# The triangular solve of a delta-rule recurrence: operand turned in 32x32 squares on VectorE instead of on TensorE, 32x64 tiles instead of 64x64, and the work around it reordered

## The chip, the cores and the metric

The kernel runs on one core of one Trainium2 chip. The metric is the device time of one execution in microseconds, as a median over runs. Beside it stands one profiled execution with its trace. All data is float32, apart from the routing tables.

## The reference

Two layers follow one another on an input x of 8 sequences x 512 steps x 256 channels (16 heads of 16).

```python
xx = pad(x)[:, :T] - x;  mix = x + xx * time_maa_x
lo = tanh(mix @ maa_w1) ...;  xm = x + xx * (lo @ maa_w2 + time_maa)      # four mixed inputs
r, k, v = xrg @ Wr.T, xk @ Wk.T, xv @ Wv.T                                  # and gates w, a, ma, mk, g
def step(s, (q, w, k, v, a, b)):            # s: 16x16 state per head and sequence
    sa = s @ a
    s = s * w + outer(sa, b) + outer(v, k)
    return s, s @ q
y = groupnorm(scan(step)) * ln_w + ln_b + (sum(r * k * faaaa)) * v
x1 = (y * g) @ Wo.T                          # first layer; the kernel adds x and normalises per token
# second layer: tokens are routed to 1 of 8 experts by argmax(x1 @ centroids.T);
# layernorm, relu(x W1[e] + b1[e]) W2[e] + b2[e], added to the token and written in token order
```

The scan is computed in blocks of 32 steps. Inside a block the effect of the steps on one another is a unit triangular 32x32 system per sequence and head (128 systems per block). Its inverse U is computed on GpSimd, and the solution X = U R is a set of small matrix products on TensorE, where R is what the state and the values contribute at each step.

## The kernel before

**Stages.** There are 16 blocks of 32 steps. `body(n)` is written once for each of the five engine queues and is called for n = -2 to 18. In one call it works on several blocks at once: projections and gates of block n+1, values of block n, solve, read-out and state update of block n-1, projection of the output and token statistics of block n-2, router of block n-3. After the loop the routing table is made, and the expert stage runs over 39 groups of 128 token slots. Each engine works strictly through its own list; the order on an engine is the order of the calls in its `body`, and engines wait for one another by semaphore counts.

**Names.** Channels lie in two halves f of 128 partitions; each half has four pairs of heads p (32 partitions each), and a group g is one half of one of the 8 sequences (16 groups). Two PSUM tensors `RY` (even and odd sequences) collect R and Y; six further PSUM banks are handed round by `Ring`: its list gives for each job the bank (`z@1` is job z in bank 1), and a job may start only when the job before it in that bank was read (`freed`).

**Around the solve.** TensorE's `read_state` puts R in `RY`. VectorE's `keep_r` copies it with a mask for even and odd heads to `Rm`; TensorE's `turn_r` turns it in 8 transposes of 128x128 (line 654); ScalarE's `keep_rt` copies the result to `RT`; `solve(m, f)` (line 699) multiplies, for each half f, 32 matrices `Ux` of 64x64 (two inverses on a block diagonal, zeros beside them) with 32 columns of `RT`. `keep_x` (ScalarE, line 1153) and `keep_x_odd` (VectorE, line 1505) copy X beside the values to `XV`, which `update` (line 716) and `read_out` (line 728) use.

**Around the inverse.** SyncE's `scores_to_pairs` writes the masked scores to DRAM (`scr_n`, line 462), loads them as one system per partition (line 467); GpSimd's `invert` works on them (it begins with the memset of line 1896); `inverse_to_heads` stores the result (`scr_u`, line 475) and loads it into `Ux` in four parts (line 486). Its place on SyncE is behind `store_x1` (line 452) and `load_tokens` (line 444).

**Around the scores.** VectorE's `mask_removal` (line 1467) and `mask_keys` (line 1436) fill `bkm` for all groups, then `difference` (1362) and `mix_stage` (1369) prepare the inputs of block n+2, then `keep_scores` (1489) reads each bank of scores. TensorE's `low_1` needs the mix, and `scores(n+1, 1)` goes into banks that `keep_scores` of the first half has to have read.

Of the kernel before, what the change touches and what calls it, by code (L numbers as in the profile page):

```python
# [143 lines left out]
def build(nc, d, out):  # L144
    with ExitStack() as ctx:
# [59 lines left out]
        def prm(name, h):  # L205
# [34 lines left out]
        Ux = [v.rearrange("p (f g k h t) -> p f g k h t", f=HALF, g=PAIRS, k=4, h=2)  # L240
              for v in (Ux_flat[:, 0:2048], Ux_flat[:, 2048:4096])]
        at_rm = top[0]
        Rm_flat = take(NB // 2 * P)
        Rm = Rm_flat.rearrange("p (g o h t) -> p g o h t", g=NB // 2, o=2, h=2)
        RT = [take(4 * P).rearrange("p (k n) -> p k n", k=4) for _ in range(HALF)]
# [37 lines left out]
        def within_words(v):  # L283
            at = [0]

            def some(words):
# [28 lines left out]
        nd = nc.dram_tensor("scr_n", (HALF, PAIRS, 4, 2, 2 * TB, TB), F32, kind="Internal").ap()  # L315
# [16 lines left out]
        proj = Stage(sem("proj"), [(1, "k z0 z1 a0 a1 sg ma0 ma1 abs sq sab mk0 mk1 ln lnss inv W ek iW0 iW1 v "  # L332
                                        "vm0 vm1 tg")])
        comb = Stage(sem("comb"), [(1, "kk scan t f k2 ls e2 kkn q ao bt k3 rk bm0 bm1 km0 km1 u wend")])
# [8 lines left out]
        chain_dve = Stage(sem("chain_dve"), [(-1, "rme rmo x1o x0o")])  # L343
        state_dve = Stage(sem("state_dve"), [(-1, "sa s")])
        chain_act = Stage(sem("chain_act"), [(-1, "rt1 rt0 x1e x0e ye yo")])
# [8 lines left out]
                 "r": [(comb, "rk"), (comb, "q")], "v": [(proj, "v"), (proj, "vm1")], "kk": [(comb, "kk")], "ss": [(comb, "bm1")],  # L354
                 "rk": [(comb, "u")], "rt0": [(chain_act, "rt0")], "rt1": [(chain_act, "rt1")], "su": [(state_dve, "s")],
# [6 lines left out]
        freed.update({f"x{f}": [(chain_act, f"x{f}e"), (chain_dve, f"x{f}o")] for f in range(HALF)})  # L362
        filled = [sem(f"filled{i}") for i in range(len(banks))]
        ring = Ring(banks, [(0, "bk00@5"), (1, "h@2 k@3"), (0, "bk01@2"), (1, "z@1 a@4 kk@5"), (-3, "logit@2"),
# [40 lines left out]
        block = ctx.enter_context(nc.Block())  # L405
        x_rows_of = lambda e: slice(64 * (1 - e), 64 * (1 - e) + 64)
# [4 lines left out]
        def _(sp):  # L411
            w = Waits(sp, carrier)

            early = [(masks, d["masks"]), (mats, d["mats"].rearrange("m p n -> p m n"))]
# [40 lines left out]
            def scores_to_pairs(m):  # L455
# [3 lines left out]
                for f in range(HALF):  # L459
                    score.wait(sp, m, *(f"sc{f}{p}" for p in range(PAIRS)))  # L460
                    for e in range(2):
                        sp.dma_start(nd[f, :, :, e].rearrange("g k r t -> r g k t"),
                                     sc[m % 2][x_rows_of(e), f, :, :, e, 0, :]).then_inc(n_out, 16)
# [3 lines left out]
                sp.dma_start(Up[m % 2].rearrange("p r c -> p (r c)"),  # L467
                             nd.rearrange("f g k e (h s) t -> (f g k e h) (s t)", h=2)).then_inc(n_in, 16)

            def inverse_to_heads(m):  # L470
# [5 lines left out]
                if m == last:  # L476
                    load_tokens(last)
                sp.wait_ge(u_out, (m + 1) * 16)
                if m == 0:
                    sp.wait_ge(clear_ok, 1)  # L480
                if m >= 2:
                    ring.wait_full(sp, m - 2, "x0", "x1")
                for e in range(2 if m < last else 1):
                    for h in range(2):
                        at_row = 64 * (1 - e) + TB * h
                        sp.dma_start(Ux[m % 2][at_row:at_row + TB, :, :, :, h, :], u_rows[e, h]).then_inc(u_in, 16)

            u_rows = ud.rearrange("(f g k e h) (r c) -> e h r f g k c", f=HALF, g=PAIRS, k=4, e=2, r=TB)
# [1528 lines left out]
```

## Time and profile before

| | us |
|---|---|
| median of 3 runs | 1094.39 |
| lowest and highest | 1082.82, 1096.72 |
| the profiled execution | 1087.63 |
| its span, first to last instruction | 1085.4 |

In that execution TensorE (PE) is busy for 93% of the span, VectorE (DVE) for 72%, GpSimd (POOL) for 57% and ScalarE (ACT) for 50%. The loop over blocks takes the time to about 750 us, the expert stage the rest.
### The profile page before, as it was taken

What the parts mean: (1) busy time and instruction counts of PE and PEld (TensorE: products, weight loads), DVE (VectorE), ACT (ScalarE), POOL (GpSimd) and SP (SyncE); (2) the same over time, 40 slices, a digit from 0 to 9 for tenths busy, and PEclk for the clock granted to TensorE, in tenths of its full rate; (3) what the DMA queues carried; (4) which work ended last, traced back from release to release, by engine and by line L of the source; (5) the groups of instructions that cost most, each with busy time, mean ns of one, the idle gap of its engine ahead of it and who ended that gap; (6) DMA issues with size and microseconds to landing.
All of it is one profiled execution on the core that took longest, in us unless ns stands there. A gap on an engine that the chain in (4) does not pass through costs nothing.

```text
span 1085.4 us, 42536 instructions
## 1 busy us (share of the span) xinstructions
PE 1010.8 (93%) x16804; PEld 833.9 (77%) x16805; DVE 777.0 (72%) x1777; ACT 542.0 (50%) x1113; POOL 614.4 (57%) x1135
## 2 busy tenths in 40 slices
PE   8898999999999999999999999499899999999995
PEld 5676777787777787777777777477799888989894
DVE  4776788788887887888788777157467666666663
ACT  4475677686685685776766766122122222222220
POOL 1088786787687885876867868820223232333321
PEclk9999999999999999999999999689999999999998
DMA  4113224234134133243242242828555454545430
GB/s 110 42 20 79 72 43 99 58 56 110 40 73 109 27 86 87 37 99 82 41 100 59 54 101 44 234 63 289 182 182 181 148 185 150 189 144 182 150 125 4
DMA packets 208752, 112.15 MB, mean 103 GB/s; under 512 B 172364, under 2 KB 192080, under 8 KB 208208
## 3 DMA queue, kind: packets, MB, share of 16 engines
q1 hardware_dynamic: 202208, 100.90, 34.4%
q0 software_dynamic: 3744, 8.40, 2.3%
q8 instruction: 122, 2.00, 0.8%
q10 hardware_dynamic: 2640, 0.54, 0.3%
q14 instruction: 38, 0.31, 0.1%
HBM read 85.55 MB, written 26.08 MB: 103 GB/s over the span
## 4 chain that ended last, share of the span: by engine, by line
PE 78%; DMA 7%; DVE 6%; issue 5%; ACT 1%; SPq 1%; POOL 1%; DVEq 1%; POOLq 0%; ACTq 0%
PE bank L561 19%; PE bank L950 12%; PE bank L963 9%; PE bank L646 6%; PE bank L699 6%; PE bank L654 5%; PE ry L963 4%; PE bank L607 3%; PE ry L676 2%; PE ry L728 2%; PE bank L716 2%; DMA arena<-scr_n 2%; DMA scr_n<-arena 2%; DMA arena<-scr_u 2%; DVE arena L1489 1%
## 5 line engine op out<-in xcount | busy, mean ns | idle before, releaser
L1906 POOL TENSOR_TENSOR arena<-arena 128x30 f32<-128x30 f32 (+14 forms) x480 | 263.5, 549 | 37.6
L561 PE MATMUL bank<-arena 128*128 128x256 f32 (+2 forms) x992 | 266.5, 406 | 5.9 <-DVE arena L1405 2.5
L1903 POOL TENSOR_TENSOR arena<-arena 128x30 f32<-128x30 f32 (+14 forms) x480 | 249.9, 521 | 36.4
L561 PEld LDWEIGHTS bank<-arena 128*128 128x128 f32 x992 | 172.7, 196 | 50.9 <-issue 24.7
L950 PEld LDWEIGHTS bank<-arena 128*128 128x128 f32 x1248 | 146.9, 194 | 5.5 <-issue 2.7
L950 PE MATMUL bank<-arena 128*128 128x128 f32 x1248 | 147.4, 277 | 3.1 <-DVE arena L1812 2.5
L1489 DVE TENSOR_TENSOR arena<-bank,arena 128x512 f32<-128x512 f32 x128 | 79.5, 682 | 32.8 <-PE bank L646 32.8
L1293 ACT ACTIVATE arena<-arena 128x1 f32<-128x1 f32 x39 | 11.5, 295 | 177.2 <-DVE arena L1766 177.2
L963 PE MATMUL bank<-arena 128*128 x416 | 96.4, 385 | 0.0
L1937 POOL COPY arena<-arena 128x1 int32 (+1 forms) x39 | 7.1, 183 | 146.2 <-DVE arena L1830 146.2
L963 PEld LDWEIGHTS bank<-arena 128*128 128x128 f32 x416 | 76.9, 190 | 14.4 <-issue 4.8
L699 PEld LDWEIGHTS bank<-arena 64*64 64x64 f32 x2048 | 65.3, 140 | 24.2 <-issue 16.7
L654 PE MATMUL bank<-arena 128*128 128x128 f32 x560 | 80.9, 281 | 2.0 <-issue 0.9
L699 PE MATMUL bank<-arena 64*64 64x32 f32 x2048 | 68.5, 224 | 14.2 <-DMA arena<-scr_u 12.1
L654 PEld LDWEIGHTS bank<-arena 128*128 128x128 f32 x560 | 64.9, 143 | 19.3 <-issue 13.6
L646 PE MATMUL bank<-arena 32*128 32x64 f32 x2048 | 69.0, 275 | 9.4 <-issue 8.5
L1931 POOL DMA_INDIRECT arena<-scr_x,arena x39 | 41.2, 1056 | 61.1 <-POOL arena L1929 30.4
L646 PEld LDWEIGHTS bank<-arena 32*128 32x128 f32 x2048 | 63.8, 188 | 13.7 <-issue 11.5
L1380 DVE SCALAR_TENSOR_TENSOR bank<-bank,arena 128x256 f32<-128x256 f32 x128 | 56.1, 483 | 22.4 <-PE bank L579 22.4
L1896 POOL MEMSET arena<- 128x32 f32 x16 | 2.5, 157 | 121.1 <-DMA arena<-scr_n 121.1
L1812 DVE TENSOR_SCALAR arena<-bank,arena 128x128 f32<-128x128 f32 x156 | 44.0, 344 | 23.1 <-issue 18.0
L1939 POOL DMA_INDIRECT out_dram<-arena x39 | 39.8, 1021 | 34.9 <-DVE arena L1796 20.8
(174 smaller groups left out, 1799.2 us busy)
## 6 DMA issues: line engine op xcount, KB each, us to landing
arena<-in_W SPq DMA_DIRECT2D x47, 1024.0 KB, 5.0
scr_n<-arena SPq DMA_DIRECT2D x64, 128.0 KB, 3.0
arena<-scr_n SPq DMA_DIRECT2D x16, 512.0 KB, 3.9
scr_u<-arena SPq DMA_DIRECT2D x16, 512.0 KB, 2.9
arena<-scr_u SPq DMA_DIRECT2D x62, 128.0 KB, 2.8
arena<-in_xTp SPq DMA_DIRECT2D x32, 132.0 KB, 4.1
arena<-in_x SPq DMA_DIRECT2D x64, 64.0 KB, 2.1
scr_x<-arena SPq DMA_DIRECT2D x64, 64.0 KB, 2.5
```

Of the source, the lines that this page charges most:

```text
L561: mm = pe.matmul(ring.tile(m, name)[0:rows, to], lhsT, rhs, start=(i == 0), stop=(i == len(terms) - 1))
L646: mm = pe.matmul(ring.tile(m, f"sc{f}{p}")[:, b * 2 * TB:(b + 1) * 2 * TB], bkm[r, f * B + b, :], aq[m % 2][r, f * B + b].rearrange("p x t ...
L654: mm = pe.transpose(ring.tile(m, name)[:, i * P:(i + 1) * P], src, ident)
L699: mm = pe.matmul(ring.tile(m, f"x{f}")[x, at:at + 32], Ux[m % 2][x, f, p, k].rearrange("p h t -> p (h t)"), RT[f][x, k, 32 * p:32 * p + 32 ...
L950: mm = pe.matmul(hidT_ps[t // 4][:, (t % 4) * P:(t % 4 + 1) * P], W1[s][:, k, t * P:(t + 1) * P], xnT[:, k, :], start=(k == 0), stop=(k == ...
L963: mm = pe.matmul(y_ps[s][:, 0:D], hidT[s][:, t, :], W2f[:, bass.ds(e * (FT * D) + t * D, D)], start=(t == 0), stop=(t == FT - 1))
L1380: xm_ok.inc(m, f"{g}{h}", STT(out=part, in0=part, scalar=prm(f"maa{g}", h), in1=dx[:, h], op0=ALU.add, op1=ALU.mult))
L1489: score.inc(m, name, TT(sc[m % 2][:, f, p].rearrange("p k e x t -> p (k e) (x t)"), ring.tile(m, name)[:, :].rearrange("p (b n) -> p b n", ...
L1812: relu_dve.inc(str(t), nc.vector.tensor_scalar(hidT[s][:, t], hidT_ps[1][:, (t - 4) * P:(t - 3) * P], b1f[:, bass.ds(e * FT + t, 1)], 0.0, ...
L1903: inv_ok.inc(f"m{s}", TT(t, U[:, 0:s, s:s + 1].broadcast_to(shape), U[:, s:s + 1, s + 1:TB].broadcast_to(shape), ALU.mult))
L1906: inv_ok.inc(f"a{s}", TT(U[:, 0:s, s + 1:TB], U[:, 0:s, s + 1:TB], t, ALU.add))
L1931: nc.gpsimd.indirect_dma_start(out=xg[:, s], out_offset=None, in_=x_rows, in_offset=bass.IndirectOffsetOnAxis(ap=index, axis=0), bounds_ch ...
```

## The change

- **R.** `keep_r` is now two VectorE transposes that turn each 32x32 square of R where it stands, into `Rs`. `turn_r`, `keep_rt`, `Rm` and `RT` are gone.
- **Solve.** `solve(m, w)` now multiplies matrices of 32 rows and 64 columns (two inverses side by side) with 32 columns of `Rs`; the products of a head with the other head's R also arise, and are masked when X is copied. Two pairs of heads are worked on in each call, alternately into banks `xa` and `xb`; both are complete only after `solve(m, 1)`. There are again 64 matmuls per block.
- **Copies of X.** Three VectorE multiplications with a mask, and two ScalarE copies with a scale of 0 or 1; `x_kept` waits for all of them.
- **Order and banks.** `gates`, then a and kk ahead of z, `ma_mk` ahead of the router; both parts of the solve behind `project_out`, with `norms` between them. `Ring` has other banks.
- **Masked keys** are written for each half apart, and the scores and the transposes of keys of a half wait for that half alone.
- **SyncE** stores the inverse first, then issues the token loads, then the loads of the inverse, then the store of x1 of block n-3.

TensorE's list, from the second transposes of keys to the first read-out of X, in a middle block. Before (L607 is z, a, kk, ma, mk; L769 a filling matmul; L561 128x8 the router, x2 behind it the gates; L654 x8 `turn_r`; L561 x4 `project_out`; L699 the solve; L561 128x512 `norms`; then r, keys, v):

```order
L607 MATMUL bank<-arena 128x256 x6
L769 MATMUL bank<-arena 128x256
L561 MATMUL bank<-arena 128x8 x4
L561 MATMUL bank<-arena 128x256 x2
L607 MATMUL bank<-arena 128x256 x4
L654 MATMUL bank<-arena 128x128 x8
L561 MATMUL bank<-arena 128x256 x4
L699 MATMUL bank<-arena 64x32 x32
L561 MATMUL bank<-arena 128x512
L561 MATMUL bank<-arena 128x256 x4
L699 MATMUL bank<-arena 64x32 x32
L654 MATMUL bank<-arena 128x128 x12
```

Now:

```order
L572 MATMUL bank<-arena 128x256 x2
L618 MATMUL bank<-arena 128x256 x10
L789 MATMUL bank<-arena 128x256
L572 MATMUL bank<-arena 128x8 x4
L572 MATMUL bank<-arena 128x256 x4
L714 MATMUL bank<-arena 64x32 x32
L572 MATMUL bank<-arena 128x512
L714 MATMUL bank<-arena 64x32 x32
L572 MATMUL bank<-arena 128x256 x4
L666 MATMUL bank<-arena 128x128 x12
```

The eight transposes are gone; the second part of the solve moved from behind r, keys and v to ahead of them, with one 128x512 matmul between the two parts.

VectorE's list, from the key exponent to the scores. Before (L1505 the copies of X, L1467 and L1436 the masks, L1362 and L1369 the inputs of the next block, L1489 the scores):

```order
L1505 COPY arena<-bank 64x4x128
L1403 SCALAR_TENSOR_TENSOR arena<-arena 128x512
L1405 SCALAR_TENSOR_TENSOR arena<-arena,bank 128x512
L1425 TENSOR_TENSOR arena<-bank,arena 128x512
L1505 COPY arena<-bank 64x4x128
L1467 TENSOR_TENSOR arena<-bank,arena 128x8x2x32 x2
L1436 TENSOR_TENSOR arena<-arena 128x8x2x32 x2
L1369 SCALAR_TENSOR_TENSOR arena<-arena 128x256 x2
L1489 TENSOR_TENSOR arena<-bank,arena 128x512 x4
```

Now:

```order
L1411 SCALAR_TENSOR_TENSOR arena<-arena 128x512
L1413 SCALAR_TENSOR_TENSOR arena<-arena,bank 128x512
L1512 TENSOR_TENSOR arena<-bank,arena 64x2x8x32 x3
L1433 TENSOR_TENSOR arena<-bank,arena 128x512
L1477 TENSOR_TENSOR arena<-bank,arena 128x4x2x32 x2
L1445 TENSOR_TENSOR arena<-arena 128x4x2x32 x2
L1377 SCALAR_TENSOR_TENSOR arena<-arena 128x256 x2
L1499 TENSOR_TENSOR arena<-bank,arena 128x512 x4
```

Between the rows shown stand others that did not change. The two copies of X, one ahead and one behind, became three in one place, and each mask is now written in two pieces (the second pair, like the first, is not shown).

SyncE's list, one block, before and now:

```order
L462 DMA scr_n<-arena 64x16x32 x4
L467 DMA arena<-scr_n 128x1024
L452 DMA scr_x<-arena 32x2x256 x4
L444 DMA arena<-in_x 32x2x256 x4
L475 DMA scr_u<-arena 128x1024
L486 DMA arena<-scr_u 32x32x32 x4
```

```order
L474 DMA scr_n<-arena 64x16x32 x4
L479 DMA arena<-scr_n 128x1024
L487 DMA scr_u<-arena 128x1024
L456 DMA arena<-in_x 32x2x256 x4
L498 DMA arena<-scr_u 32x32x32 x4
L464 DMA scr_x<-arena 32x2x256 x4
```

The store of the inverse now stands directly behind the load of the next systems. The core of the diff:

```diff
+        Rs = take(NB * TB).rearrange("p (e g i) -> p e g i", e=2, g=NB // 2)
+        head_mask = take(TB + 2)
...
-        ring = Ring(banks, [(0, "bk00@5"), (1, "h@2 k@3"), (0, "bk01@2"), (1, "z@1 a@4 kk@5"), (-3, "logit@2"),
-                            (-2, "g@0"), (1, "ma@5 mk@2"), (-1, "rt0@3 rt1@4"), (-2, "wo@0"), (-1, "x1@1"),
-                            (1, "ss@0 r@4"), (0, "bk11@5"), (1, "v@2"), (-1, "x0@3"), (0, "bk10@5 v0@1 v1@4"),
-                            (1, "rk@3"), (-1, "su@0"), (1, "sc00@2 sc01@5 sc02@3 sc03@1 tg@4"), (2, "lo1@5"),
+        ring = Ring(banks, [(0, "bk00@5"), (1, "h@2 k@3"), (0, "bk01@2"), (-2, "g@4"), (1, "a@5 kk@3 z@1 ma@4 mk@2"),
+                            (-3, "logit@3"), (-2, "wo@0"), (1, "ss@0"), (-1, "xa@1 xb@3"), (1, "r@4"),
+                            (0, "bk11@5"), (1, "v@2"), (0, "bk10@5 v0@1 v1@3"),
+                            (1, "rk@4"), (-1, "su@0"), (1, "sc00@2 sc01@5 sc02@3 sc03@1 tg@4"), (2, "lo1@5"),
...
+            def solve(m, w):
+                if w == 0:
+                    for bank in "ab":
+                        ring.wait_empty(pe, m, f"x{bank}")
+                    chain_dve.wait(pe, m, "re", "ro")
+                    pe.wait_ge(u_in, (m + 1) * 64)
+                else:
+                    pe.wait_ge(half_solved, m + 1)
+                for g in range(NB // 2):
+                    for turn in range(2):
+                        for i, bank in enumerate("ab"):
+                            e, r = (turn + i) % 2, pair_rows(2 * w + i)
+                            at = (w * NB // 2 + g) * 32
+                            mm[bank] = pe.matmul(ring.tile(m, f"x{bank}")[x_rows_of(e), at:at + 32],
+                                                 Ux[m % 2][r, g % 4, g // 4, e].rearrange("p h t -> p (h t)"), Rs[r, e, g, :],
+                                                 start=True, stop=True)
...
             def keep_r(m):
...
                 for e, name in enumerate("eo"):
-                    chain_dve.inc(m, f"rm{name}", TT(Rm[:, :, 1 - e], RY[e][:, :, 0, None, :].broadcast_to(shape),
-                                                     odd_even[:, None, :, None].broadcast_to(shape), ALU.mult))
+                    chain_dve.inc(m, f"r{name}", nc.vector.transpose(Rs[:, e], RY[e][:, :, 0]))
+            def keep_x(m, bank, e):
+                ring.wait_full(dve, m, f"x{bank}")
+                chain_dve.inc(m, f"x{bank}{'eo'[e]}", TT(solution_home(m, "ab".index(bank), e), solution(m, f"x{bank}", e),
+                                                         same_head[x_rows_of(e), None, None, :].broadcast_to([P // 2, 2, NB // 2, 32]),
+                                                         ALU.mult))
```

## Rows read from the trace of the kernel before

**Rows 1.** A block by engine: busy PE, PEld, DVE, ACT, POOL; PEclk, DMA share, GB/s.
```profile
333.00:373.40 40.40, 39.10 (x919) 31.42 (x918) 34.75 (x61) 29.58 (x55) 31.36 (x60) 1.00 0.33 74
```

**Rows 2.** Time line of GpSimd: where the inverses of block 1, of a middle block and of the last begin.
```profile
90.34 0.16 POOL L1896 MEMSET arena<- 128x32 f32 x1 [1.85 <-DMA arena<-scr_n]
...
342.18 0.16 POOL L1896 MEMSET arena<- 128x32 f32 x1 [4.57 <-DMA arena<-scr_n]
...
679.41 0.15 POOL L1896 MEMSET arena<- 128x32 f32 x1 [3.17 <-DMA arena<-scr_n]
```

**Rows 3.** Time line of TensorE in one block, 332 to 374 us.
```profile
332.02 1.12 PE L561 MATMUL bank<-arena 128*128 128x512 f32 x2
...
348.70 1.09 PE L654 MATMUL bank<-arena 128*128 128x128 f32 x8
...
351.45 2.06 PE L699 MATMUL bank<-arena 64*64 64x32 f32 x64
...
361.83 0.76 PE L728 MATMUL ry<-arena 128*32 128x32 f32 x64
...
365.16 0.68 PE L728 MATMUL ry<-arena 128*32 128x32 f32 x54 [0.69 <-issue]
...
370.54 2.01 PE L646 MATMUL bank<-arena 32*128 32x64 f32 x62
...
373.41 1.12 PE L561 MATMUL bank<-arena 128*128 128x512 f32 x2
```

**Rows 4.** Groups of TensorE by line and shape, 119 to 680 us: busy, mean ns, idle before.
```profile
L646 PE MATMUL bank<-arena 32*128 32x64 f32 x1728 | 59.0, 275 | 9.1 <-issue 8.5 <-DVE arena L1489 0.3
L699 PE MATMUL bank<-arena 64*64 64x32 f32 x1664 | 53.4, 220 | 2.4 <-DMA arena<-scr_u 2.4
L728 PE MATMUL ry<-arena 128*32 128x32 f32 x1664 | 21.2, 199 | 5.7 <-issue 5.7
```

**Rows 5.** Time line of VectorE in the same block.
```profile
343.48 1.28 DVE L1499 TENSOR_TENSOR arena<-ry,arena 128x512 f32<-128x512 f32 x2
...
354.35 0.92 DVE L1403 SCALAR_TENSOR_TENSOR arena<-arena 128x512 f32<-128x512 f32 x1
...
355.92 0.69 DVE L1452 SCALAR_TENSOR_TENSOR bank<-bank,arena 128x512 f32<-128x512 f32 x1
...
360.49 0.68 DVE L1505 COPY arena<-bank 64x512 f32<-64x512 f32 x1 [0.47 <-PE bank L699]
361.09 1.27 DVE L1467 TENSOR_TENSOR arena<-bank,arena 128x512 f32<-128x512 f32 x2
362.29 1.92 DVE L1436 TENSOR_TENSOR arena<-arena 128x512 f32<-128x512 f32 x2
...
366.06 1.38 DVE L1369 SCALAR_TENSOR_TENSOR arena<-arena 128x256 f32<-128x256 f32 x2
367.94 2.48 DVE L1489 TENSOR_TENSOR arena<-bank,arena 128x512 f32<-128x512 f32 x4 [0.51 <-PE bank L646]
```

**Rows 6.** VectorE, 119 to 680 us by line: its slowest operation on 512 elements.
```profile
L1391 DVE TENSOR_TENSOR_SCAN arena<-arena,bank 128x512 f32<-128x512 f32 x13 | 15.8, 1212 | 0.0
```

**Rows 7.** Time line of VectorE at the end of the loop: operations on 224 and 256 elements.
```profile
730.44 0.38 DVE L1602 COPY arena<-bank 128x224 f32<-128x224 f32 x1
...
751.01 0.43 DVE L1708 TENSOR_TENSOR arena<-arena 128x256 f32<-128x256 f32 x1
```

**Rows 8.** Time line of SyncE's queue in the same block.
```profile
343.33 0.37 SPq L475 DMA_DIRECT2D scr_u<-arena  x1
346.20 2.22 SPq L486 DMA_DIRECT2D arena<-scr_u  x4
```

**Rows 9.** A stretch of two us by engine, as rows 1.
```profile
326.00:328.00 2.00, 2.00 (x9) 1.52 (x7) 1.70 (x3) 0.00 (x0) 1.76 (x4) 0.50 0.00 0
```

**Rows 10.** Time line of ScalarE in the same block.
```profile
350.05 0.60 ACT L1148 ACTIVATE arena<-bank 128x512 f32<-128x512 f32 x1
...
353.69 0.63 ACT L1097 ACTIVATE arena<-arena 128x512 f32<-128x512 f32 x1
```

More of the change, by code:

```diff
@@ L477, in inverse_to_heads @@
                     load_tokens(last)
+                elif m and m - 1 < last - 1:
+                    load_tokens(m - 1)
                 sp.wait_ge(u_out, (m + 1) * 16)
@@ L481, in inverse_to_heads @@
                 if m >= 2:
[L482 to L488, printed above, removed]
+                    ring.wait_full(sp, m - 2, "xa", "xb")
+                for p in range(PAIRS if m < last else 2):
+                    sp.dma_start(heads_of(m, p), u_rows[p]).then_inc(u_in, 16)
             def load_experts(some):
                 ring.wait_full(sp, last, "sc03", "sc13", "tg", "k", "r", "v")
-                comb.wait(sp, last, "u", "ao", "bm1", "km1", "q", "wend")
+                comb.wait(sp, last, "u", "ao", "bm11", "km11", "q", "wend")
                 if some.stop == E:
@@ L508, in body @@
             def body(n):
-                if has(n - 2) and n - 2 < last - 1:
-                    load_tokens(n - 2)
                 if has(n - 1):
                     inverse_to_heads(n - 1)
+                if has(n - 3) and n <= last:
+                    store_x1(n - 3)
                 if n == last:
@@ L522, in body @@
                     load_tokens(last - 1)
-                if has(n - 2):
+                if has(n - 2) and n >= last:
                     store_x1(n - 2)
@@ L793, in body @@
                     turn_keys(n, 0, 1)
+                if has(n - 2):
+                    gates(n - 2)
+                if n == last + 2:
+                    keep_busy(2, idle_ps)
                 if has(n + 1):
@@ L805, in body @@
                 if has(n - 2):
-                    gates(n - 2)
-                if n == last + 2:
-                    keep_busy(2, idle_ps)
+                    project_out(n - 2)
+                if has(n - 1) and n - 1 < last:
+                    solve(n - 1, 0)
                 if has(n + 1):
-                    ma_mk(n + 1)
+                    norms(n + 1)
                 if -1 <= n <= 0:
-                    keep_busy(4, ry_bank[0])
-                if has(n - 1):
-                    turn_r(n - 1, 0)
-                    turn_r(n - 1, 1)
-                if has(n - 2):
-                    project_out(n - 2)
+                    keep_busy(1, ry_bank[0])
                 if n == last + 2:
@@ L822, in body @@
                 if n == last + 1:
-                    ring.wait_empty(pe, last, "x1")
+                    ring.wait_empty(pe, last, "xa")
                     keep_busy(2, idle_ps)
+                if n - 1 == last:
+                    solve(n - 1, 0)
                 if has(n - 1):
                     solve(n - 1, 1)
-                if has(n + 1):
-                    norms(n + 1)
-                if -1 <= n <= 0:
-                    keep_busy(1, ry_bank[0])
                 if has(n + 1):
@@ L838, in body @@
                     keep_busy(3, ry_bank[0])
-                if has(n - 1):
-                    solve(n - 1, 0)
                 if has(n) and n < last:
@@ L1062, in keep_k @@
                 if m:
[L1063 removed]
+                    comb.wait(act, m - 1, "rk", "km11")
                 ring.wait_full(act, m, "k")
@@ L1229, in body @@
                     abs_of_z(n + 1)
+                if has(n - 3):
+                    keep_logits(n - 3)
                 if n == last + 1:
-                    odd_inverse_to_heads(last)
-                if has(n - 1):
-                    keep_rt(n - 1, 1)
+                    second_inverse_to_heads(last)
                 if has(n + 1):
@@ L1244, in body @@
                     decays(n + 1)
+                if has(n - 1):
+                    keep_x(n - 1)
                 if has(n) and n < last:
                     keep_keys(n, 1, 1)
-                if has(n - 1):
-                    keep_rt(n - 1, 0)
                 if has(n + 1):
@@ L1657, in body @@
                     bonus_terms(n + 1)
-                if has(n - 1):
-                    keep_x_odd(n - 1, 0)
                 if has(n + 1):
-                    mask_removal(n + 1)
-                    mask_keys(n + 1)
+                    for f in range(HALF):
+                        mask_removal(n + 1, f)
+                        mask_keys(n + 1, f)
                     bonus_values(n + 1)
```

155 lines of the change are left out of this document (75 added, 80 removed).

## The prediction

> **What bounds the kernel now.** I read the stretches first. In a block of the loop TensorE is busy 39.1 of 40.4 us and VectorE 34.75 [rows 1]: TensorE sets the pace, but VectorE has only about 5.6 us to spare, in pieces. Next I read how long a block is: GpSimd begins an inverse once per block, and from block 1 to block 15 these starts lie 589.07 us apart, 42.08 us for each of 14 blocks [rows 2]. GpSimd isn't the bound: it waits 3 to 5 us for each block's input [rows 2], so its own work is some 37 us a block, and that is the floor for any gain. The chain of waits of the shown block runs through TensorE's list almost without a break.
>
> The time line of the block shows two things more. From one centring matmul to the next (332.02 to 373.41) it takes 41.4 us [rows 3]. And TensorE stands still for "issue", that is for nothing that the profile names, mostly in the stretches of tiny matmuls: 0.69 us in this block's read-out, 8.5 and 5.7 us in total on the lines of scores and read-out over thirteen blocks [rows 3, 4].
>
> VectorE is the close second where the block ends. Its inputs for the next block are done at 366.06 + 1.38 = 367.44, and it starts reading scores at 367.94, when TensorE delivers them [rows 5]. TensorE in its turn can't start the second half of the scores until three of the first four banks are read. So whatever TensorE saves ahead of this place is gained only as far as VectorE comes earlier too.
>
> **What the change takes off TensorE.** (a) Eight transposes take 1.09 us per block [rows 3]: about -1.0 without the overlap with their neighbours. (b) The solve is 64 matmuls before and after. 32 of them with 64x64 weights take 2.06 us, 64 ns each; two lie side by side in the array, so each place takes 128 ns [rows 3]. The new tiles are 64 columns wide as well, but only 32 rows high, and four successive ones lie in four different places. Bounds: 64 ns each as now (no gain), or the 24 ns of the 128x32 tiles, 0.76 us for 32 [rows 3], which would make it 1.5 instead of 4.1 us. I take 128 ns over four places, 32 ns, because the weights keep their width: 2.06 us for both parts, a saving of 2.06. Together TensorE has 3.1 us less per block.
>
> Here the trace and a rule differ. The 32 matmuls of a read-out use all rows of the array and only differ in columns, and yet follow one another every 24 ns, far less than their 199 ns each [rows 3, 4]. The Trainium skill, "TensorE: Matmul & The Clock Gate", Part 3, says that weights load during a running matmul only when the row group differs; by that, tiles that share rows would not overlap, and (b) would be worth nothing. That case is rival two below; the row speaks against it.
>
> **What it adds on VectorE, and where.** I follow VectorE from the key exponent on. (c) The key exponent begins at 354.35 because the logarithm on ScalarE begins at 353.69 [rows 5, 10]. ScalarE loses a copy of 0.6 us ahead of it (`keep_rt`, at 350.05) [rows 10], and a and z no longer stand around the router's logits; I estimate 1.0 us earlier. (d) Three copies of X in one place cost 3 x 0.62 (a quarter of the 2.48 us of four reads of 512 elements [rows 5]) = 1.9 us; so the work that began at 355.92 begins at 355.92 - 1.0 + 1.9 = 356.8. The solve begins at 351.45 - 1.0 = 350.4 and is done after 1.0 + 1.1 + 1.0 us (a 128x512 matmul between its parts, the row at 373.41 [rows 3]), at 353.6, so the copies don't wait. (e) The copy at 360.49 goes, with its wait: 0.47 + 0.6 us [rows 5]; now 0.2 earlier than before. (f) The four masks begin at 361.09, the last two at 362.29 and take 1.92: 3.1 us [rows 5]. Eight halves have 256 elements each. Bounds: half the time each (nothing added), or the full time each (3.1 us added). An operation on 224 elements from PSUM took 0.38 us, one on 256 elements from SBUF 0.43 [rows 7]; I take 4 x 0.37 + 4 x 0.45 = 3.3 us, 0.2 added. (g) `keep_r` took 1.28 us [rows 5]; two transposes of 256 elements lie between 2 x 0.38 [rows 7] and 2 x 1.21, the slowest operation on this engine [rows 6]. I take 0.8 to 0.9, nearest to the size; it matters little, since VectorE waits for the gates and for sigma right behind it.
>
> So VectorE has the next inputs ready at 367.4, as before, and now TensorE is waiting for them: its first scores would be done 3.1 us earlier. `low_1` waits some 2.5 us for the mix. The reads of scores begin at 367.4 instead of 367.94, the third is done at 369.3, and the second half of the scores starts at 369.4 instead of 370.54; it is 2.0 us long, and the centring matmul comes at 371.4 instead of 373.41 [rows 3]. The block is 39.4 us long, 2.0 less. The issue gap of 0.69 us no longer costs anything, as it now lies in front of a wait. Gaps in other places stay. I take 1.9 us per block; 1.2 of the 3.1 us are given back.
>
> **The other parts.** SyncE stores the inverse at 343.33, though GpSimd had finished at 342.18 - 4.57 = 337.6 [rows 2, 8]: 5.7 us late, behind x1 and the tokens. The store now goes at once, and the loads of `Ux` (issued from 346.20 on) come some 5 us earlier. This was waited for in only 2.4 us over thirteen blocks [rows 4], so it gains 0.2 us a block at most; it is what keeps a shorter block and an earlier solve from waiting for the inverse. The four token loads are issued while the store lands, and are needed only when `project_out` is done. The store of x1 goes a block later, with nobody behind it but the loads of x, which VectorE needs only behind the masks [rows 5]. ScalarE has less to do. The other banks put `ma` behind the gates, the router behind the sum of kk, and `norms` behind the token sum; each is free 0.5 us or more before TensorE comes, but `norms` only just. I cost these at nothing; if VectorE is a us late there, they cost that us.
>
> **Sum.** 14 blocks x 1.9 = 26.6, and about 1 us for the last solve, which stands in the open: 1087.63 - 27.6 = 1060.0, against the profiled execution's own time. The median of the runs is 6.8 above that execution, one run was 4.8 below it. I shift by 1: **1061 us**.
>
> **Rivals.**
> 1. *TensorE's gain comes through whole.* VectorE also gets faster by its earlier inputs and TensorE never waits at `low_1`. For it: VectorE's 5.6 us of idle time. Against: the place where it is needed has 0.5 us of it [rows 5]. (3.1 + 0.2) x 14 + 1 = 47: 1041. Chance 0.13.
> 2. *The smaller tiles are no faster.* Then only (a) is saved, X is complete 2 us later, and the three copies of X, which begin at about 354.8, wait 1.1 us. The block is 0.8 shorter: 14 x 0.8 = 11: 1076. Chance 0.10.
> 3. *The clock.* Five stretches of the loop run at a granted clock of 0.50, that is 1.2 GHz, for some four us around 100, 200, 326, 412 and 538 us; one of them is shown [rows 9]. TensorE was busy throughout before each, in the small matmuls of read-out and scores. A wait of 2.5 us in just that place makes it less busy. If it happened in each block, nine more times at about 1.7 us: 15 of the 27 us are gone, 1076. Chance 0.12. Against: part of a slower stretch would lie ahead of a wait.
> 4. *VectorE becomes the bound, and the kernel is slower.* The mechanism is (f) and (d): if an operation's cost is mostly fixed, or strides cost, the eight half masks take 3.1 us more instead of 0.2 and the three copies up to 1.21 us each, 1.8 more. With 4 us more per block than I take, 14 x (4 - 1.9) = 29: 1117. From 1.9 us on the gain is gone, from 3.5 on it is over 2% slower. Against: rows 7. Chance 0.07.
>
> My forecast's chance is 0.58, its own range 1051 to 1072 (1.1 to 2.6 us a block, which covers (f) at 0 to 0.8 us more, and runs that differ by several us).
>
> **Numbers.** The range reaches into rivals 1 to 3: 1040 to 1083. Two per cent, about what a measurement of this kernel can tell from no change, is 22 us, so "faster" ends at 1072.5. Rival 1 and nearly all of my case are below: 0.62. The rest of it and rivals 2 and 3: 0.31. Rival 4: 0.07.
>
> **What would show it.** The starts of inverses 40.2 us apart on average, 38 to 39 if TensorE alone decides, 41.3 if the tiles are no faster. The solve: 32 matmuls in 1.0 us. VectorE's transposes near 0.4 us each, half masks near 0.4 to 0.45. TensorE idle ahead of `low_1` (the 128x256 matmuls between the two halves of the scores), released by VectorE's mix. SyncE's store of the inverse within half a us of GpSimd's end, and no wait of the solve for `scr_u`. Wrong would be: waits at `norms`, `ma` or the router for VectorE, a solve at 64 ns per matmul, or more than eight stretches at the lower clock.

## The result

The changed kernel takes 1108.73 us (median of 4 runs, 1106.85 to 1117.75) where the kernel before took 1093.45 us in the same comparison: ratio 1.0189, interval 1.0143 to 1.0236. I had forecast 1061 and a range that ended at 1083. The profiled execution took 1108.01 us, its span is 1106.0. The ratios here and below leave out executions over 1.5% longer than the fastest of the same kernel: seven of ten in e4, two of ten in e8, one of ten in e10.

### The profile page after: what moved, and what is told of

Same layout as the page of the kernel before. It is cut to its first block, busy times and chain, and to the rows that moved or that the text cites. A ratio compares the mean times of both kernels' runs of the same rounds, so it can differ in the third digit from the quotient of the medians.

```text
span 1106.0 us, 42284 instructions
## 1 busy us (share of the span) xinstructions
PE 997.4 (90%) x16676; PEld 813.9 (74%) x16677; DVE 792.8 (72%) x1857; ACT 519.8 (47%) x1081; POOL 606.6 (55%) x1135
## 4 chain that ended last, share of the span: by engine, by line
PE 63%; DVE 15%; issue 7%; POOL 6%; DMA 5%; ACT 2%; DVEq 2%; SPq 1%; ACTq 0%; POOLq 0%
PE bank L572 17%; PE bank L969 9%; PE bank L982 9%; PE bank L658 6%; PE bank L618 4%; PE bank L714 3%; POOL arena L1916 3%; POOL arena L1913 3%; PE ry L982 3%; DVE arena L1445 2%; PE ry L688 2%; PE bank L666 2%; PE bank L736 2%; DVE arena L1477 2%; PE ry L694 2%
## 5 line engine op out<-in xcount | busy, mean ns | idle before, releaser
L572 PE MATMUL bank<-arena 128*128 128x256 f32 (+2 forms) x992 | 283.7, 423 | 18.7 <-DVE arena L1433 10.4
L1916 POOL TENSOR_TENSOR arena<-arena 128x30 f32<-128x30 f32 (+14 forms) x480 | 259.3, 540 | 37.6
L1913 POOL TENSOR_TENSOR arena<-arena 128x30 f32<-128x30 f32 (+14 forms) x480 | 246.5, 514 | 36.4
L572 PEld LDWEIGHTS bank<-arena 128*128 128x128 f32 x992 | 180.6, 204 | 59.4 <-issue 16.7
L969 PEld LDWEIGHTS bank<-arena 128*128 128x128 f32 x1248 | 145.2, 192 | 5.6 <-issue 2.9
L969 PE MATMUL bank<-arena 128*128 128x128 f32 x1248 | 145.9, 275 | 3.1 <-DVE arena L1822 2.5
L982 PEld LDWEIGHTS bank<-arena 128*128 128x128 f32 x416 | 76.9, 190 | 14.4 <-issue 4.9
L658 PE MATMUL bank<-arena 32*128 32x64 f32 x2048 | 79.5, 307 | 6.8 <-issue 6.8
L658 PEld LDWEIGHTS bank<-arena 32*128 32x128 f32 x2048 | 74.3, 218 | 10.7 <-issue 8.5
L666 PE MATMUL bank<-arena 128*128 128x128 f32 x432 | 61.9, 277 | 4.4 <-issue 1.8
L666 PEld LDWEIGHTS bank<-arena 128*128 128x128 f32 x432 | 51.5, 143 | 18.8 <-issue 12.5
L714 PEld LDWEIGHTS bank<-arena 32*64 32x64 f32 x2048 | 37.3, 146 | 30.4 <-issue 22.2
L1316 ACT ACTIVATE arena<-bank,arena 128x128 f32<-128x128 f32 x156 | 44.6, 369 | 25.2 <-PE bank L969 25.2
```

The lines of the kernel that those rows point to most:

```text
L572: mm = pe.matmul(ring.tile(m, name)[0:rows, to], lhsT, rhs, start=(i == 0), stop=(i == len(terms) - 1))
L658: mm = pe.matmul(ring.tile(m, f"sc{f}{p}")[:, b * 2 * TB:(b + 1) * 2 * TB], bkm[r, f * B + b, :], aq[m % 2][r, f * B + b].rearrange("p x t ...
L666: mm = pe.transpose(ring.tile(m, name)[:, i * P:(i + 1) * P], src, ident)
L714: mm[bank] = pe.matmul(ring.tile(m, f"x{bank}")[x_rows_of(e), at:at + 32], Ux[m % 2][r, g % 4, g // 4, e].rearrange("p h t -> p (h t)"), R ...
L969: mm = pe.matmul(hidT_ps[t // 4][:, (t % 4) * P:(t % 4 + 1) * P], W1[s][:, k, t * P:(t + 1) * P], xnT[:, k, :], start=(k == 0), stop=(k == ...
L982: mm = pe.matmul(y_ps[s][:, 0:D], hidT[s][:, t, :], W2f[:, bass.ds(e * (FT * D) + t * D, D)], start=(t == 0), stop=(t == FT - 1))
```

## The profile after

This is the time line of GpSimd in the changed kernel, with the starts of the inverses of block 1, of a middle block and of the last; it answers to [rows 2].

```profile
93.20 0.16 POOL L1906 MEMSET arena<- 128x32 f32 x1 [4.28 <-DMA arena<-scr_n]
...
311.72 0.15 POOL L1906 MEMSET arena<- 128x32 f32 x1 [6.58 <-DMA arena<-scr_n]
...
697.90 0.15 POOL L1906 MEMSET arena<- 128x32 f32 x1 [6.02 <-DMA arena<-scr_n]
```

The 14 blocks take 604.70 us instead of 589.07: 43.2 us a block, 15.6 of the 20.4 us that the two profiled executions differ by. The rest is 2.9 us ahead of block 1 and 2 behind the last start.

Next the loop by engine (busy time of PE, PEld, DVE, ACT, POOL with instructions, clock, DMA share, GB/s), first of the kernel before, then of the changed one.

```profile
90.00:679.00 589.00, 559.93 (x12820) 443.56 (x12819) 473.14 (x819) 410.62 (x763) 452.43 (x854) 0.99 0.32 70
```

```profile
93.00:698.00 605.00, 549.87 (x12702) 428.56 (x12701) 487.11 (x887) 390.15 (x732) 445.04 (x856) 0.93 0.31 68
```

TensorE is busy for only 10 us less, though by the prediction some 43 us of work were taken off (14 x 3.1), and it is idle for 55 us instead of 29. The granted clock is 0.93 instead of 0.99. So there are two things: the clock, and waits. The time line of TensorE in one block shows both (it answers to [rows 3]; L714 is the solve, L748 and L736 read-out and update, L572 x4 behind the read-out the bonus, L658 the scores):

```profile
404.11 1.13 PE L714 MATMUL bank<-arena 32*64 32x32 f32 x64
...
412.69 0.76 PE L748 MATMUL ry<-arena 128*32 128x32 f32 x64
414.40 1.10 PE L572 MATMUL bank<-arena 128*128 128x256 f32 x4 [0.95 <-DVE arena L1433]
417.24 1.08 PE L736 MATMUL bank<-arena 128*32 128x32 f32 x64 [1.74 <-DVE arena L1477]
418.08 1.09 PE L748 MATMUL ry<-arena 128*32 128x32 f32 x64
419.11 3.69 PE L658 MATMUL bank<-arena 32*128 32x64 f32 x64
422.73 3.78 PE L572 MATMUL bank<-arena 128*128 128x256 f32 x8
```

The solve is nearly as fast as I took it (1.13 us for 32 matmuls, 1.03 forecast). But TensorE waits 0.95 us for the bonus terms and 1.74 us ahead of the first update, neither of which I had forecast, and from there its work takes up to twice its time: 3.69 us for scores that took 2.01 [rows 3]. Here are two stretches of 2 us in that place (columns as above):

```profile
416.00:418.00 2.00, 0.76 (x57) 0.79 (x61) 2.00 (x5) 1.90 (x5) 1.76 (x4) 0.69 0.00 0
420.00:422.00 2.00, 2.00 (x48) 2.00 (x44) 0.99 (x2) 0.00 (x0) 1.83 (x3) 0.50 0.00 0
```

These are two of TensorE's waits from 119 to 690 us (sum, times, longest):

```profile
PE bank L736 <- DVE arena L1477: 22.9, 13, 1.8
PE bank L572 <- DVE arena L1433: 9.7, 13, 1.3
```

Each comes once in each of the 13 blocks. The first is the wait for a bank: `su` (the update) and `ss` (the norms, later the removal) share bank 0, and `ss` is free only when VectorE has written the last masked removal, `bm11`. VectorE's time line shows why that is late (it answers to [rows 5]; L1508 the transposes of R, L1512 the copies of X, L1477 half removals, L1445 half keys):

```profile
310.29 0.77 DVE L1508 STREAM_TRANSPOSE arena<-ry 128x256 f32<-128x256 f32 x2
...
321.54 2.01 DVE L1512 TENSOR_TENSOR arena<-bank,arena 64x512 f32<-64x512 f32 x3
...
327.45 0.74 DVE L1477 TENSOR_TENSOR arena<-bank,arena 128x256 f32<-128x256 f32 x2
328.11 1.59 DVE L1445 TENSOR_TENSOR arena<-arena 128x256 f32<-128x256 f32 x2
329.62 0.74 DVE L1477 TENSOR_TENSOR arena<-bank,arena 128x256 f32<-128x256 f32 x2
330.29 1.17 DVE L1445 TENSOR_TENSOR arena<-arena 128x256 f32<-128x256 f32 x2
```

The keys of the first half now stand between the two halves of the removal, and they are slow. By line, 119 to 690 us:

```profile
L1445 DVE TENSOR_TENSOR arena<-arena 128x256 f32<-128x256 f32 x52 | 38.9, 787 | 0.0
L1477 DVE TENSOR_TENSOR arena<-bank,arena 128x256 f32<-128x256 f32 x52 | 19.3, 411 | 0.0
L1508 DVE STREAM_TRANSPOSE arena<-ry 128x256 f32<-128x256 f32 x26 | 10.0, 421 | 0.0
```

SyncE stores the inverse 0.8 us after GpSimd's end (311.72 - 6.58 = 305.14), not 5.7 [rows 8], and the solve hardly waits for it (0.2 us from 119 to 690 us, 2.4 before):

```profile
305.91 0.39 SPq L487 DMA_DIRECT2D scr_u<-arena  x1
```

## The experiments

The theories: **W**, TensorE's waits among its smallest matmuls let the granted clock fall, and cost more than their length. **T**, the smaller tiles and the lighter work let it fall, wherever TensorE waits. **V**, VectorE's work between solve and scores sets the block. "Lost clock" below is the time of the 14 blocks at 1.2 GHz, halved, read in stretches of 1 us from the start of inverse 1 to that of inverse 15, in one profiled execution of each. It is an upper estimate of what the clock costs, since TensorE doesn't work in all of that time; what the clock did cost shows in TensorE's busy time for the same matmuls. Each ratio is against runs of the kernel before that were taken with the run, so small differences between rows are read from the ratios.

| run | ratio to before (interval) | median | 14 blocks | stretches, lost clock | waits of bonus and first update for VectorE |
|---|---|---|---|---|---|
| before | 1 | | 589.1 | 5, 8.5 | 0 |
| the change | 1.019 (1.014 to 1.024) | 1108.7 | 604.7 | 12, 45.0 | 9.7 + 22.9 |
| e1 removal first | 1.002 (0.998 to 1.005) | 1093.1 | 587.7 | 8, 20.4 | 7.9 + 2.7 |
| e5 before, half masks | 1.013 (1.008 to 1.018) | 1105.8 | 600.9 | 7, 15.3 | 0 + 2.0 |
| e3 solve twice | 1.059 (1.052 to 1.065) | 1153.1 | 644.9 | 11, 40.9 | 1.5 + 19.2 |
| e6 whole masks | 0.987 (0.978 to 0.995) | 1075.4 | 570.8 | 5, 15.3 | 9.5 + 0 |
| e12 keys first | 1.023 (1.018 to 1.029) | 1114.4 | 608.0 | 14, 51.2 | 9.8 + 27.4 |
| e13 the same, filled | 1.013 (1.009 to 1.017) | 1104.5 | 602.3 | 7, 25.6 | 1.3 + 3.9 |
| e10 old queue order in e6 | 1.005 (1.001 to 1.009) | 1097.9 | 594.9 | 11, 30.7 | 5.0 + 0 |

**e1, the order of the half masks.**

```diff
                     for f in range(HALF):
                         mask_removal(n + 1, f)
+                    for f in range(HALF):
                         mask_keys(n + 1, f)
```

> The changed kernel with one thing moved: VectorE writes both halves of the masked removal first, then both halves of the masked keys, so that the bank of `ss`, which the state update needs, is free 1.5 us earlier. Theory W (TensorE's waits of 1 and 1.7 us ahead of the bonus and the first update, among its smallest matmuls, make the granted clock fall): the wait ahead of the update falls from 1.75 to under 0.5 us a block, the stretches at 1.2 GHz in the loop from 12 to 8 or fewer, the time by 15 to 30 us to about 1080 to 1093. Theory T (the clock falls because the turned operand and the 32x64 tiles leave TensorE with less and smaller work, wherever it waits): the stretches stay 11 or more, and the time falls only by part of the wait, 5 to 15 us.

The kernel takes 1093.1 us, at the edge of W's band: 15.6 us less by moving two instructions of VectorE ahead of two others. The wait ahead of the update is nearly gone (2.7 us), and with it more than half of the lost clock. T falls: the tiles are the same. The loop of e1 by engine:

```profile
94.00:682.00 588.00, 535.40 (x12700) 412.33 (x12698) 489.99 (x887) 389.03 (x731) 443.44 (x855) 0.97 0.33 70
```

Set beside the loop of the change, TensorE is busy 14.5 us less for the same matmuls and idle only 2.5 us less (52.6 instead of 55.1). The wait for VectorE went elsewhere: matmuls behind the first half of the scores wait 10.4 us in all, 7 times, for VectorE's reads of scores; in the change it was 1.8 us, 3 times. So most of what e1 wins is the clock.

**e2 and e7, filling matmuls.** One ahead of `bonus`, three behind it:

```diff
+                    ring.wait_empty(pe, n + 1, "sc00")      # e7: "sc01"
+                    keep_busy(1, ring.tile(n + 1, "sc00"))
                 if has(n + 1):
                     bonus(n + 1)
+                    keep_busy(3, ring.tile(n + 1, "sc00"))
```

> The changed kernel with four filling matmuls of 128x128x256, 1.9 us of work that nobody needs, per block where TensorE waits: one ahead of the bonus, three ahead of the first update. Theory W: the waits are filled, the granted clock stays up (5 stretches or fewer at 1.2 GHz), and although TensorE has more work the time falls to 1070 to 1085. Theory T: the same number of tiles is as small as before, the clock still falls in 8 or more blocks, the time stays within 10 us of 1109. If the lost time were the waits themselves and not the clock: no change.

e2 takes 1112.7 us (1.019, 1.011 to 1.026): no gain, and outside W's band. The filling itself waited 27 us for ScalarE's copies of the values in that bank, so the design was poor.

> As the run with filling matmuls, but into the bank of the key transposes, which ScalarE has read by then, so that the filling doesn't wait for ScalarE itself: one ahead of the bonus, three ahead of the first update, 1.9 us where TensorE waits 2.5. Theory W (the clock falls because of the waits): lost clock falls from 45 us to 15 or less, the waits to under 1 us a block, and the time to 1085 to 1100. If the clock costs nothing of its own because slow stretches lie ahead of VectorE's waits anyway: 1105 to 1112 with a clock that is up.

e7 takes 1100.2 us (1.011, 1.003 to 1.019), at the upper edge of W's band: 27 us of useless work added, and the kernel some 8 us faster. The two intervals overlap, so this run alone doesn't show the gain. Lost clock only fell to 25.6 us, not to 15; the waits fell to 2.8 + 5.8 us.

**e3, the solve twice.**

```diff
-                for g in range(NB // 2):
+                for g in [g for g in range(NB // 2) for _ in range(2 if 0 <= m < last else 1)]:
```

> The changed kernel with each of the solve's 64 matmuls issued twice (same result written twice), 2.1 us more of 32x64 tiles per block. Theory W: TensorE comes later to the bonus and the update by up to 2 us, VectorE's copies of X somewhat too (1 us), so the waits shrink but do not vanish; fewer stretches (6 to 10) and a time within 12 us of 1109 or below it. Theory T: more of the small tiles, more stretches at 1.2 GHz (12 or more) and 25 to 30 us longer.

Here both theories missed. The wait for the bonus terms fell from 9.7 to 1.5 us, but the one ahead of the update only from 22.9 to 19.2. A later solve makes VectorE's copies of X late, and with them everything to `ss`: 2.1 us of work cost 2.9 us a block (644.9 against 604.7), which fits a path from the solve through VectorE; no run shows that path apart. The kernel is 44 us slower, beyond T's 25 to 30 as well, and twice as many small tiles brought no more lost clock (40.9 against 45.0), which speaks against T. The 64 matmuls of one part took 2.07 us, 32 ns each again.

**e5, half masks in the kernel before.**

```diff
-                    mask_removal(n + 1)
-                    mask_keys(n + 1)
+                    for f in range(HALF):
+                        mask_removal(n + 1, f)
+                        mask_keys(n + 1, f)
```

> The kernel before with one part of the change alone: masked removal and masked keys by halves, in the order removal 0, keys 0, removal 1, keys 1, TensorE waiting for its half. Everything else, solve in 64x64 tiles and transposes on TensorE included, is as before. Theory W: VectorE's eight half masks take some 1.2 us longer, `ss` is free 1.5 us later, TensorE waits ahead of the first update up to 1 us, and the clock falls in 7 or more blocks instead of 5: 1098 to 1115. Theory T: the clock falls as often as before (5), and the time is within 8 us of before.

The half masks alone cost 1.3% (1105.8 us, within W's band), though TensorE hardly waits at the update (2.0 us). From 93 to 694 us TensorE is busy for 566.2 us, 6.3 more than in the loop of the kernel before, and idle for 34.8, 5.7 more; 3.6 us of waiting are for VectorE's work ahead of the scores. So about half of the loss goes with the clock and half with VectorE's longer list.

**e6, whole masks in the changed kernel** (four instructions as before, all else as changed).

> The changed kernel with the masked removal and keys in four whole instructions as before, everything else as changed. VectorE has 1.2 us a block less, `ss` is free early. If VectorE's list sets the pace (theory V: each us on VectorE between the copies of X and the scores is a us of the block): 15 us under the run with the removal first, 1075 to 1083. If it is only the early release of `ss` that counts: 1090 to 1096, as with the removal first.

e6 takes 1075.4 us, in the band of V. The half masks cost 33 us, and without them the change is 1.3% faster than before (interval 0.5 to 2.2%). About half of e6's lost clock lies in one stretch in block 1, around a wait of 4.2 us of the solve for `scr_u`. This is the best kernel of the study, with e9.

**e12, keys ahead of removal in e6.** No engine has anything more to do.

```diff
-                    mask_removal(n + 1)
                     mask_keys(n + 1)
+                    mask_removal(n + 1)
```

> Against the run with whole masks (1075): the same four instructions of VectorE, but the keys ahead of the removal. No engine has a nanosecond more to do; only the bank of `ss` is free 1.9 us later, and TensorE waits for it ahead of the first update, next to its smallest matmuls. Theory W (a wait there costs itself and lets the granted clock fall): the wait there goes from under 0.2 to 1.5 us or more a block, the lost clock from 15 us to 30 or more, the time by 15 to 30 us to 1090 to 1105. Theory V (only VectorE's work on the way to the scores counts; the wait is a wait in another place): within 8 us of 1075.

e12 takes 1114.4 us, 39 us more and beyond W's band. The loop of e6 and then of e12 by engine:

```profile
94.00:665.00 571.00, 529.39 (x12699) 408.64 (x12696) 473.96 (x831) 389.31 (x730) 450.79 (x856) 0.97 0.34 72
```

```profile
93.00:701.00 608.00, 550.81 (x12699) 430.59 (x12700) 473.26 (x831) 389.20 (x731) 448.44 (x854) 0.92 0.32 67
```

The same 12699 matmul records are busy 21.4 us longer, which is the clock, and TensorE is idle 57.2 instead of 41.6 us, 15.6 us more, which is waiting. Every run agrees on the clock: averaged over a whole execution it is 0.964 to 0.973 in the four runs of e6 and 0.927 to 0.936 in the four of e12. In e12 the place looks so:

```profile
410.83 0.76 PE L748 MATMUL ry<-arena 128*32 128x32 f32 x64
412.39 1.10 PE L572 MATMUL bank<-arena 128*128 128x256 f32 x4 [0.80 <-DVE arena L1433]
415.56 1.08 PE L736 MATMUL bank<-arena 128*32 128x32 f32 x64 [2.07 <-DVE arena L1475]
416.40 1.09 PE L748 MATMUL ry<-arena 128*32 128x32 f32 x64
```

**e13, e12 with the wait filled** (one filling matmul ahead of `bonus`, four behind, in the bank of e7).

> The run with the keys first (1114, 2.1 and 0.75 us of wait a block, 51 us lost to the clock), with five filling matmuls of 0.47 us where TensorE waits: one ahead of the bonus, four ahead of the first update. The bank of `ss` is released as late as there. If the clock costs time of its own (theory W): lost clock 51 to 25 or less, the time 8 to 20 us lower, 1094 to 1106. If only the wait counts and the clock is a bystander: no gain, 1112 to 1120, as the filling is 2.35 us and the waits are 2.85.

e13 is 10 us faster with 33 us more work, and the bank is released as late: the clock costs time of its own. The gain is small but clear of noise (1.009 to 1.017 against 1.018 to 1.029), and the clock of its ten executions is 0.956 to 0.967. The place in e13:

```profile
414.82 1.89 PE L789 MATMUL bank<-arena 128*128 128x256 f32 x8
417.14 0.75 PE L736 MATMUL bank<-arena 128*32 128x32 f32 x64 [0.43 <-DVE arena L1480]
```

The update takes 0.75 us here, 1.08 in e12.

**e4 and e8, the bonus later** (behind the second read-out; e4 with half masks, removal first, e8 with whole masks).

> The changed kernel with the removal masks ahead of the key masks, as in the run before, and TensorE's bonus matmuls moved from ahead of the first update to behind the second read-out. If TensorE's remaining wait of 0.7 us for the bonus terms is lost time: 0.7 us x 14 and a few us of clock, 1078 to 1088. If VectorE's list sets the end of the block (inputs of the next block ready too late), the wait only moves to the first matmuls of the block after next and the time stays within 5 us of 1093.

> Whole masks and the bonus behind the second read-out. Theory V: as the run with whole masks alone, within 4 us, since TensorE only waits elsewhere. If the two waits add up: 5 to 12 us faster than that run, 1066 to 1076.

The ratios are 1.001 (0.995 to 1.008) and 1.002 (0.998 to 1.007). The ten runs of e4 spread from 1081.9 to 1109.5 us with a median of 1101.2, so it tells only that nothing was won. e8 is 1.6% worse than e6, a miss for both theories as stated. The bonus is 1.1 us of large matmuls between read-out and update. Without it TensorE is at the update earlier and waits there for `ss`, right behind the small matmuls: 24.9 us in 13 blocks in e8's profiled execution, which at 1110.3 us was the slowest of ten. That would be the kernel of e12 by another way, but no quicker execution of e8 was profiled.

**e9, one copy of X on ScalarE** (e6, with `xbo` written by two ScalarE copies).

> Whole masks, and one of VectorE's three masked copies of X given to ScalarE as two copies of 32 partitions' worth more (0.8 us there, 0.65 us less on VectorE ahead of the bonus terms). Theory V: each us of VectorE between solve and scores is a us of the block, so 0.65 x 14 = 9 us less, and the wait of 0.75 us for the bonus terms falls to 0.1: 1062 to 1070. If the place isn't VectorE's but ScalarE's (growths late), or the copies of X on ScalarE now come last: 1073 to 1080.

e9 takes 1076.0 us (0.986, 0.982 to 0.990), the second band and no gain over e6. The wait for the bonus terms fell from 9.5 to 2.9 us, but the scores waited 2.8 us for ScalarE's value copies (0.7 in e6), and lost clock was 22.2 us instead of 15.3. V is not enough here.

**e10, SyncE's old order in e6**, and **e15, its new order in the kernel before**.

> Whole masks, and SyncE's list as before the change (tokens, inverse, x1 of the block just made). The prediction costed this part at 0.2 us a block at most. But the earlier and faster solve comes 1 us earlier: if the late inverse is now waited for, the solve waits for `scr_u` 0.5 to 1.5 us a block and the time is 1080 to 1092; if not, 1075 to 1079.

> The kernel before with SyncE's new order alone. By the prediction's 0.2 us a block: 1088 to 1091 against 1091, no difference that can be told. If the late inverse, or the x1 and token transfers ahead of it, cost the old kernel too: 1078 to 1086.

e10 takes 1097.9 us against e6's 1075.4, some 22 us more. e15 takes 1086.3 us (0.999, 0.995 to 1.003), nothing that can be told. In e10 the solve waits again:

```profile
PE bank L712 <- DMA arena<-scr_u: 11.4, 9, 2.1
```

The lost clock is twice that of e6. Only the faster kernel needs the early inverse.

**e11, eight idle transposes in the old ones' place in e6.**

> Whole masks, with eight transposes of 128x128 that nobody needs where the old ones stood, 1.0 us of TensorE's work per block ahead of the solve. If TensorE's saving from the transposes is what the change gains (as in the sum): 14 x 1.0 = 14 us slower, 1087 to 1092. If VectorE sets the block and the saved time turned into waits: the wait for the bonus terms takes 0.3 to 0.7 us of it and the clock falls less often, 1076 to 1084.

e11 takes 1084.1 us (0.994, 0.990 to 0.997), just at the end of the second band: 14 us of work cost some 9, though its interval and e6's overlap.

**e14, one filling matmul in e6**, ahead of the bonus.

> The best kernel so far (whole masks, 1075) with one filling matmul of 0.47 us ahead of the bonus, where TensorE still waits 0.75 us. Theory W: the wait falls to 0.3 us, nothing gets later, and 5 to 8 us of the 15 us of lost clock come back: 1068 to 1074. If the filling delays the bonus in blocks without a wait: 1076 to 1080.

e14 takes 1079.7 us (0.990, 0.986 to 0.994): no gain over e6, and a loss of 4 us that is within noise. This is a miss for W. The wait fell from 9.5 to 0.9 us, yet the profiled execution has 8 stretches and 27.3 us of lost clock, and the clock of twelve executions, 0.950 to 0.968, is no higher than in e6. Five of the eight stretches begin at the end of a gap, or within 2 us behind it, of 0.85 to 2.5 us among scores and read-out that the profile puts down to nothing ("issue"), and which filling doesn't reach. So the waits for VectorE are one occasion for the clock to fall and not the only one.

## Why the prediction was wrong

- **(a), (b), (g) held.** The tiles take 1.13 us for 32 matmuls where I took 1.03, and stood at 32 ns each when doubled; the transposes took 0.77 us where I took 0.8 to 0.9. The prediction cites a rule of the Trainium skill, "TensorE: Matmul & The Clock Gate", Part 3: weights load during a running matmul only when the row group differs. This trace does not agree with it: the 32 matmuls of a read-out share all rows, differ in columns, and again took 0.76 us together.
- **The step that failed first** is the sentence on the other banks, "each is free 0.5 us or more before TensorE comes". I looked at `ma`, the router and `norms`, which the diff moves, and not at `su`, whose neighbour `ss` stayed and was only released by another instruction. In the kernel before it was free at about 362.3 and needed at 363.6; with TensorE 3 us earlier and the release behind the first half of the keys, both of its sides moved the wrong way. e1 undoes the second side: 15.6 us. The wait for the bonus terms was in my own times too: done at 360.0 in the kernel before, they would come 0.9 us later (360.9), while TensorE would be at the bonus 3.1 us earlier (359.4). It measured 9.7 us in 13 blocks. The rows of the kernel before:

```profile
359.33 0.69 DVE L1425 TENSOR_TENSOR arena<-bank,arena 128x512 f32<-128x512 f32 x1
362.52 1.13 PE L561 MATMUL bank<-arena 128*128 128x256 f32 x4
363.58 0.76 PE L716 MATMUL bank<-arena 128*32 128x32 f32 x64
```

- **The wait was put in the wrong place.** I had TensorE wait 2.5 us at `low_1` for the mix. Neither the change nor e6 shows a wait for the mix.
- **(f) was mis-sized.** I took 0.45 us per half mask of keys from a plain 256-element operation. They measure 0.79, against 0.98 for a whole one: 3.2 us instead of 1.8 for four. Half masks of removal are 0.41, near what I took. Splitting adds 1.5 us a block where I had 0.2. The order and the splitting together, e6 against the change, are 33 us.
- **Rival 3 was the right mechanism with a wrong size.** I gave it nine more stretches at 1.7 us, 15 us. There were seven more, but of up to 11 us, 45 us of lost clock instead of 8.5. It went with a wait ahead of the update, not ahead of `low_1`. One reading behind this rival was wrong: I wrote that TensorE was busy throughout before each of the five stretches of the kernel before. Each of them began within 3 us behind a gap of 1.1 to 2.1 us, four in read-out or scores and one ahead of the solve; this one stands ahead of [rows 9]:

```profile
323.56 0.28 PE L728 MATMUL ry<-arena 128*32 128x32 f32 x10 [1.16 <-issue]
```

  Two other gaps among these matmuls, of 1.2 and 1.3 us, had no stretch behind them, so what decides stays open. But the rows gave more reason to fear a wait there than the chance of 0.12 says.
- **Rival 4** (0.07) is the only one that had the kernel slower. Its condition came true in part: the half masks took 1.3 us more than I took, the three copies 2.0 us as forecast, and the clock did the rest.
- **The end of the block was reckoned too short.** I had the centring matmul 2.0 us behind the start of the second half of the scores. In the rows of the kernel before it comes 2.87 us behind it (370.54 to 373.41), and 0.62 of that is an issue gap that my sum drops without a reason, though I wrote that gaps in other places stay:

```profile
373.16 0.32 PE L646 MATMUL bank<-arena 32*128 32x64 f32 x2 [0.62 <-issue]
```

  With all of it left in, a start 1.1 us earlier (370.54 to 369.4) gives 1.1 us a block and not the 1.9 of the sum.
- **SyncE's order** I costed at 0.2 us a block at most. In the shortened block it is worth some 22 us (24 us of the 14 blocks, 1.7 us a block), as e10 shows. My own reason, that it keeps an earlier solve from waiting, was right, and I gave it no price.
- **What of the forecast stood.** With the half masks taken back the change gains 16 to 18 us of the forecast 27, in the direction forecast: 40.8 us a block, where I said 40.2. The 1.3 us a block that it gains is near the 1.1 that my working gives with the gap left in, so part of the difference is that slip. What VectorE's remaining wait for the bonus terms and the clock cost beside it stays open: e9 and e14 could not win it.

## What to carry to other kernels

When a bank or buffer is shared, list for every job that comes earlier which instruction frees its neighbour, also where the diff leaves the bank alone; splitting an instruction can move the release behind work that has nothing to do with it. And when one engine is shortened, price again every transfer and every release that was hidden before, since that slack is what the gain is taken from.

A wait of 2 us on TensorE next to its smallest matmuls cost 2.8 us a block, as the clock fell in most blocks; filling a wait of 0.7 us there (e14) won nothing.

## What was not expected of the hardware

- The granted clock fell to 1.2 GHz in 14 stretches of e12 and in 5 of e6, with the same instructions on every engine and only two pairs exchanged in VectorE's list; the same matmul records took 550.8 us instead of 529.4.
- Useless matmuls made a kernel faster: 33 us of them in e13 took 10 us off e12. In e14, in a shorter wait, they won nothing.
- In the kernel before each stretch at 1.2 GHz followed a gap of 1.1 to 2.1 us in TensorE's small matmuls or ahead of the solve, most of them gaps for which the profile names no cause.
- Halving a VectorE multiplication from 512 to 256 elements took it from 0.98 to 0.79 us where both inputs and the strided output lie in SBUF, and from 0.67 to 0.41 us where one input lies in PSUM.
- A VectorE transpose of 128x256 out of PSUM in 32x32 squares takes 0.42 us, near the 0.38 us of a copy of 224 elements out of PSUM [rows 7].
